# Sums of the first graph layer: GpSimd casts lanes of four bins, five bins are added as pairs, variances at the end

## The reference, cut to what matters

```python
hij = jnp.concatenate([h[src], h[dst]], axis=-1)
e = jnp.matmul(jax.nn.leaky_relu(jnp.matmul(hij, w), 0.2), a)
exp_e = jnp.exp(e)
denom = jax.ops.segment_sum(exp_e, src, num_segments=N)
out = jax.ops.segment_sum(h[src] * (exp_e / denom[src]), dst, num_segments=N)
x = _layernorm(x + out, axis=-1)
```

## Time and profile before

| | |
|---|---|
| median of 3 timed runs | 3259.38 us (3257.14 to 3259.6) |
| span of the profiled execution | 3274.5 us |
| TensorE, VectorE, ScalarE, GpSimd busy | 93%, 93%, 84%, 5% of the span |
| granted TensorE clock, mean | 0.968 |
| the stage of the change | from 1318 to 2184 us of the span |

### The profile page before, as it was taken

How to read it: one execution, slowest core, us unless ns; L and a number is a source line. 1 busy time by engine, 2 the same in 40 slices (tenths; PEclk the granted TensorE clock), 3 DMA queues, 4 the chain that set the end, 5 groups by cost and what they waited for, 6 DMA issues and landing times. The chain is left out here.

```text
span 3274.5 us, 101508 instructions
## 1 busy us (share of the span) xinstructions
PE 3060.7 (93%) x40072; PEld 2792.8 (85%) x40072; DVE 3045.9 (93%) x4921; ACT 2750.1 (84%) x6946; POOL 155.0 (5%) x249
## 2 busy tenths in 40 slices
PE   5777699999999999699999999989999999999996
PEld 4666677778777877699999999988999999999994
DVE  8999889999999997799999999989999999999997
ACT  6988888888888885799999999987888888888887
POOL 0000000000000000000000000000111111111110
PEclk9989899999999997799999999999999999999998
DMA  3000022222222222234333333334455545554541
GB/s 66 13 14 11 23 98 93 87 93 94 93 87 93 94 86 48 65 96 97 97 97 96 97 96 97 97 93 137 161 163 160 164 161 163 161 163 161 162 151 41
DMA packets 173823, 333.06 MB, mean 102 GB/s; under 512 B 54876, under 2 KB 109616, under 8 KB 173264
## 3 DMA queue, kind: packets, MB, share of 16 engines
q1 hardware_dynamic: 170996, 323.30, 32.5%
q10 hardware_dynamic: 2348, 3.20, 0.4%
HBM read 320.77 MB, written 5.66 MB: 100 GB/s over the span
## 5 line engine op out<-in xcount | busy, mean ns | idle before, releaser
L1009 PE MATMUL l_gathered<-xp,l_src_onehot 128*128 128x128 bf16 x7203 | 467.0, 221 | 11.2 <-DVE l_src_onehot L922 11.2
L1436 PE MATMUL l_gathered<-hp,l_onehot 128*128 128x128 bf16 x7203 | 458.5, 219 | 0.0
L704 PE MATMUL sc_z<-sc_onehot,pq 128*128 128x256 f32 (+1 forms) x2450 | 429.4, 298 | 23.3 <-DVE sc_leaky L617 18.3
L1009 PEld LDWEIGHTS l_gathered<-xp,l_src_onehot 128*128 128x128 bf16 x7203 | 407.9, 99 | 26.3 <-DVE l_src_onehot L922 11.7
L788 ACT ACTIVATE sc_leaky<-sc_z 128x1024 f32<-128x1024 f32 (+3 forms) x325 | 309.8, 953 | 143.3 <-PE sc_z L708 140.5
L617 DVE SCALAR_TENSOR_TENSOR sc_leaky<-sc_z,sc_leaky 128x1024 f32<-128x1024 f32 (+3 forms) x325 | 370.1, 1139 | 60.0 <-ACT sc_leaky L788 52.5
L847 DVE TENSOR_TENSOR l_lane<-iota_b,l_lane_pairs 128x896 bf16<-128x896 bf16 x686 | 421.0, 614 | 0.0
L1436 PEld LDWEIGHTS l_gathered<-hp,l_onehot 128*128 128x128 bf16 x7203 | 406.1, 98 | 0.4
L708 PE MATMUL sc_z<-sc_onehot,pq 128*128 128x256 f32 (+1 forms) x2450 | 400.9, 286 | 0.0
L1450 PE MATMUL l_acc<-e,l_lane_wide 128*128 128x132 f32 x2744 | 385.5, 283 | 0.3 <-ACT e L1514 0.3
L704 PEld LDWEIGHTS sc_z<-sc_onehot,pq 128*128 128x128 f32 x2450 | 344.6, 196 | 35.9 <-issue 34.5
(11 more groups left out here) (246 smaller groups left out, 6107.4 us busy)
## 6 DMA issues: line engine op xcount, KB each, us to landing
rows_got<-edge_rows_wide SPq DMA_DIRECT2D x338, 448.0 KB, 3.7
l_got<-edge_rows_src SPq DMA_DIRECT2D x343, 224.0 KB, 3.2
placed<-edge_rows SPq DMA_DIRECT2D x144, 512.0 KB, 3.7
out_dram<-X SPq DMA_DIRECT2D x12, 256.0 KB
S<-edge_rows_wide SPq DMA_DIRECT2D x5, 448.0 KB, 8.4
edge_rows<-e SPq DMA_DIRECT2D x98, 6.1 KB
edge_rows_wide<-e SPq DMA_DIRECT2D x98, 12.2 KB
sc_last_rows<-edge_rows SPq DMA_DIRECT2D x24, 64.0 KB, 3.5
```

Source lines behind the costliest of these rows:

```text
L704: nc.tensor.matmul(z[:, b, 0:nw, :], PQ[:, b0 + b, q, 0:C], hot[:, r % HOTS, b, 0, 0:nw, :], start=(b == u and q == 0), stop=False)
L1009: ins = nc.tensor.matmul(gps[:, t % 2, i * P:(i + 1) * P], hot[:, t % RING, i, :], parts[:, g * GX + i, q, :], start=(q == 0), stop=(q == 2))
L1436: ins = nc.tensor.matmul(gps[:, t % 2, i * P:(i + 1) * P], dst_hot[:, t % RING, i, :], hp[:, g * GX + i, q, 0:C], start=(q == 0), stop=(q ...
```

## The change

Of the 7 bins of a round, 5 instead of 4 are added as pairs of halves, and 2 instead of 3 in plain float32. VectorE still weighs 4 (`BANK`) and ScalarE 3. The lanes' cast is divided: GpSimd casts the first four bins (`WIDENED`), ScalarE the other three (`widen_late`, semaphore `late_wide`). Messages, halves and lanes get three buffers (`KEPT`), the source one-hot four. The table's split and the source one-hot go a round further ahead.

VectorE's order in an iteration is now: source one-hot of t+3, low halves of t-1, lane one-hot of t+1, weigh t, block work. TensorE gathers t+2 ahead of adding up t. ScalarE has weigh_late, widen_late, take_high.

At a block's end VectorE adds the two parts of `acc` to X by two additions in two rounds, without S and GpSimd; statistics of all blocks are kept, and after the last round seven instructions over all 49 blocks form mean and variance from them.

```diff
@@ -852,7 +852,7 @@
 def layer0_sums(nc, k, parts, xs, den, src_rows, e0, X, S, mean_var):
     NB, PER = NBK, NBK // GX
     R = NB * PER
-    RING, LOADS, SPLIT = 3, 4, 4
+    RING, LOADS, KEPT, SPLIT, BANK, WIDENED = 4, 5, 3, 5, 4, 4
     BY_SCALAR = (2, 4, 6)
     F32R = mybir.dt.float32r
     with Stage(nc) as ctx:
@@ -864,15 +864,15 @@
 
         s = {n: ctx.semaphore("l0_" + n) for n in (
             "chain", "scaled", "scaled_late", "part_high", "part_rest", "part_middle", "part_low",
-            "hot", "staged", "lane", "lane_wide", "gathered", "messages", "late_messages", "high", "low", "added", "taken", "summed", "stats")}
+            "hot", "staged", "lane", "lane_wide", "gathered", "messages", "late_messages", "high", "low", "late_wide", "added", "taken", "summed", "stats")}
         loaded = [ctx.semaphore(f"l0_loaded{h}") for h in range(LOADS)]
         rden = sb("rden", [P, k.NI])
         got = sb("got", [P, LOADS, GX * P], BF16)
         hot = sb("src_onehot", [P, RING, GX, P], BF16)
-        lane, lane_wide = sb("lane", [P, 2, GX, P], BF16), sb("lane_wide", [P, 2, GX, P], F32R)
+        lane, lane_wide = sb("lane", [P, KEPT, GX, P], BF16), sb("lane_wide", [P, KEPT, GX, P], F32R)
         lane_pairs = sb("lane_pairs", [P, 2, NB, 2], BF16)
-        msg, halves = sb("messages", [P, 2, GX, C]), sb("message_halves", [P, 2, SPLIT, 2, C], F32R)
-        stats = sb("stats", [P, 2, 6])
+        msg, halves = sb("messages", [P, KEPT, GX, C]), sb("message_halves", [P, KEPT, SPLIT, 2, C], F32R)
+        stats, apart = sb("stats", [P, NB, 6]), sb("apart", [P, NB])
         gps = ps("gathered", [P, 2, 1024])
         acc = ps("acc", [P, 2, 512])
 
@@ -925,74 +925,92 @@
                 def weigh(t):
                     n, g = divmod(t, PER)
                     dve.wait_ge(s["gathered"], t + 1)
-                    if t >= 2:
-                        dve.wait_ge(s["low"], t - 1)
-                    nc.vector.tensor_tensor(msg[:, t % 2, 0:SPLIT], gps[:, t % 2, 0:SPLIT * P].rearrange("p (i c) -> p i c", i=SPLIT),
-                                            e0[:, n, g * GX:g * GX + SPLIT].unsqueeze(2).to_broadcast([P, SPLIT, C]), ALU.mult
+                    if t >= KEPT:
+                        dve.wait_ge(s["low"], t - KEPT + 1)
+                    nc.vector.tensor_tensor(msg[:, t % KEPT, 0:BANK], gps[:, t % 2, 0:BANK * P].rearrange("p (i c) -> p i c", i=BANK),
+                                            e0[:, n, g * GX:g * GX + BANK].unsqueeze(2).to_broadcast([P, BANK, C]), ALU.mult
                                             ).then_inc(s["messages"], 1)
 
                 def take_low(t):
                     dve.wait_ge(s["high"], t + 1)
-                    nc.vector.tensor_tensor(halves[:, t % 2, :, 1, :], msg[:, t % 2, 0:SPLIT], halves[:, t % 2, :, 0, :], ALU.subtract
-                                            ).then_inc(s["low"], 1)
+                    nc.vector.tensor_tensor(halves[:, t % KEPT, :, 1, :], msg[:, t % KEPT, 0:SPLIT], halves[:, t % KEPT, :, 0, :],
+                                            ALU.subtract).then_inc(s["low"], 1)
 
                 def take(n):
                     dve.wait_ge(s["added"], (n + 1) * PER)
-                    nc.vector.tensor_reduce(S[:, n, :], acc[:, n % 2, 0:2 * C].rearrange("p (q c) -> p c q", q=2), AX.X, ALU.add
-                                            ).then_inc(s["taken"], 1)
+                    nc.vector.tensor_tensor(X[:, n, :], X[:, n, :], acc[:, n % 2, 0:C], ALU.add).then_inc(s["taken"], 1)
+
+                def take_rest(n):
+                    dve.wait_ge(s["taken"], n + 1)
+                    nc.vector.tensor_tensor(X[:, n, :], X[:, n, :], acc[:, n % 2, C:2 * C], ALU.add).then_inc(s["summed"], 1)
 
                 def measure(n):
                     dve.wait_ge(s["summed"], n + 1)
-                    nc.vector.bn_stats(stats[:, n % 2, :], X[:, n, :]).then_inc(s["stats"], 1)
-
-                def average(n):
-                    dve.wait_ge(s["stats"], n + 1)
-                    nc.vector.bn_aggr(mean_var[:, n, :], stats[:, n % 2, :])
+                    nc.vector.bn_stats(stats[:, n, :], X[:, n, :]).then_inc(s["stats"], 1)
+
+                def average():
+                    dve.wait_ge(s["stats"], NB)
+                    even, odd = stats[:, :, 0:3], stats[:, :, 3:6]
+                    ch.link(nc.vector.tensor_tensor(mean_var[:, :, 0], even[:, :, 1], odd[:, :, 1], ALU.add))
+                    ch.link(nc.vector.tensor_tensor(apart[:], even[:, :, 1], odd[:, :, 1], ALU.subtract))
+                    nc.vector.tensor_tensor(stats[:, :, 0], even[:, :, 2], odd[:, :, 2], ALU.add)
+                    ch.link(nc.vector.tensor_tensor(apart[:], apart[:], apart[:], ALU.mult))
+                    nc.vector.tensor_scalar(mean_var[:, :, 0], mean_var[:, :, 0], 0.5, None, ALU.mult)
+                    ch.link(nc.vector.scalar_tensor_tensor(out=apart[:], in0=apart[:], scalar=C / 4.0, in1=stats[:, :, 0], op0=ALU.mult,
+                                                           op1=ALU.add))
+                    nc.vector.tensor_scalar(mean_var[:, :, 1], apart[:], 1.0 / C, None, ALU.mult)
 
                 def find_lanes(t):
                     n, g = divmod(t, PER)
-                    if t >= 2:
-                        dve.wait_ge(s["lane_wide"], t - 1)
+                    if t >= KEPT:
+                        dve.wait_ge(s["lane_wide"], t - KEPT + 1)
+                        dve.wait_ge(s["late_wide"], t - KEPT + 1)
                     if g == 0:
                         dve.wait_ge(s["staged"], n + 1)
-                    compare_lanes(nc, k, lane[:, t % 2], lane_pairs[:, n % 2, g * GX:(g + 1) * GX, :]).then_inc(s["lane"], 1)
+                    compare_lanes(nc, k, lane[:, t % KEPT], lane_pairs[:, n % 2, g * GX:(g + 1) * GX, :]).then_inc(s["lane"], 1)
 
                 ch.link(nc.vector.tensor_scalar(den, den, 1.1754944e-38, None, ALU.max))
                 ch.link(nc.vector.reciprocal(rden[:], den))
                 scale(0)
                 scale(1)
                 part_rest(0)
-                for t in range(-2, R):
-                    c = t + 3
+                for t in range(-3, R + 1):
+                    c = t + 4
                     if c + 1 < PER and c + 1 not in BY_SCALAR:
                         scale(c + 1)
                     if c < PER:
                         part_rest(c)
                     if c - 1 < PER:
                         part_low(c - 1)
-                    if t + 2 < R:
-                        make(t + 2)
-                    if t >= 0:
-                        weigh(t)
+                    if t + 3 < R:
+                        make(t + 3)
+                    if t >= 1:
+                        take_low(t - 1)
                     if 0 <= t + 1 < R:
                         find_lanes(t + 1)
-                    if t >= 0:
-                        take_low(t)
+                    if 0 <= t < R:
+                        weigh(t)
                     if t >= PER and t % PER == 2:
                         take(t // PER - 1)
+                    if t >= PER and t % PER == 3:
+                        take_rest(t // PER - 1)
                     if t >= PER and t % PER == 4:
                         measure(t // PER - 1)
-                    if t >= PER and t % PER == 5:
-                        average(t // PER - 1)
                 take(NB - 1)
+                take_rest(NB - 1)
                 measure(NB - 1)
-                average(NB - 1)
+                average()
 
             @block.gpsimd
             def _(pool):
-                for n in range(NB):
-                    pool.wait_ge(s["taken"], n + 1)
-                    nc.gpsimd.tensor_tensor(X[:, n, :], X[:, n, :], S[:, n, :], ALU.add).then_inc(s["summed"], 1)
+                def widen(t):
+                    pool.wait_ge(s["lane"], t + 1)
+                    if t >= KEPT:
+                        pool.wait_ge(s["added"], t - KEPT + 1)
+                    nc.gpsimd.tensor_copy(lane_wide[:, t % KEPT, 0:WIDENED], lane[:, t % KEPT, 0:WIDENED]).then_inc(s["lane_wide"], 1)
+
+                for t in range(R):
+                    widen(t)
 
             @block.tensor
             def _(pe):
@@ -1014,22 +1032,23 @@
                     n, g = divmod(t, PER)
                     pe.wait_ge(s["late_messages"], t + 1)
                     pe.wait_ge(s["lane_wide"], t + 1)
+                    pe.wait_ge(s["late_wide"], t + 1)
                     if g == 0 and n >= 2:
-                        pe.wait_ge(s["taken"], n - 1)
+                        pe.wait_ge(s["summed"], n - 1)
                     for i in range(SPLIT, GX):
-                        nc.tensor.matmul(acc[:, n % 2, 0:C], lane_wide[:, t % 2, i, :].bitcast(F32), msg[:, t % 2, i, :],
+                        nc.tensor.matmul(acc[:, n % 2, 0:C], lane_wide[:, t % KEPT, i, :].bitcast(F32), msg[:, t % KEPT, i, :],
```

(41 more changed lines are left out.)

## The result

The changed kernel takes 3376.95 us in the median of 4 runs (3365.61 to 3387.06) against 3259.43; the ratio is 1.0361 (95% interval 1.0332 to 1.0389). It is 117.5 us slower, where 116 were forecast. The profiled executions differ by 3385.2 - 3274.5 = 110.7 us.

What follows compares the result with a forecast made beforehand. A closed VectorE-ScalarE loop was taken to bound the kernel, TensorE close behind. Over 338 steady rounds +112 us, start +3 and end +1 raise 3259.4 to 3375 us, 3.6% slower; range 3340 to 3470.

Steps and rivals of the forecast that it cites:

- The loop: Steady rounds: weighing, ScalarE's high halves, low halves, lane one-hot close in 2.753 us against 2.422, +112 us.
- The terms within: Pieces of a steady round: high halves 0.725 us on ScalarE; low halves 0.74 and lane one-hot 0.53 on VectorE.
- TensorE: Its work in a steady round falls by 0.08 to 2.31 us, leaving it idle some 0.4 us.
- Rival C: TensorE, idling, drops to half clock in a third of the rounds: 3586 us; chance 0.05.
- GpSimd's cast: Casting four lane bins hides in VectorE's 0.43 us idle gap and costs nothing if up to 0.94 us long.
- D: Length of GpSimd's lane cast of 512 elements: taken as 0.89 us, bounds 0.57 and 1.86.
- rival A: GpSimd's lane cast exceeds 0.94 us, each 0.1 us over costing 34 us: 3463 at 1.2 us; chance 0.20.
- Block work: Block-end additions and statistics on VectorE, each under 0.3 us, start in the 0.43 us gap and delay nothing.
- Start and end: First interleaved rounds and prologue +3 us (bounds -4 and +8); after the last round +1 us.
- Rival B: VectorE's low halves don't wait for ScalarE, rounds take 2.32 us: 3229 us; chance 0.07.

Runs made afterwards that it cites:

- lanes_before_low: The changed kernel with VectorE's lane one-hot of t+1 put ahead of the low halves of t-1: 3218.57 us, ratio 0.9882.
- scalar_casts_all: The changed kernel with all seven bins of lanes cast by ScalarE, none by GpSimd: 3370.95 us, ratio 1.0348.
- low_two_later: The changed kernel with VectorE taking the low halves of t-2 instead of t-1 in iteration t: 3325.50 us, ratio 1.0199.
- block_work_alone: The kernel before with only the change's block work (two additions from PSUM, statistics finished at the end): 3261.45 us, ratio 1.0008.
- low_two_later_scalar_casts: The changed kernel with low halves of t-2 in iteration t and all lanes cast by ScalarE: 3220.77 us, ratio 0.9882.

## Why the prediction was right

*The loop.* This step carried 112 of the 116 us, and it is shown: forecast 2.753 us a round, measured 2.753; forecast idle 0.43, measured 0.43; low halves 1.48 after the weighing, measured 1.48. `lanes_before_low` removes it by order alone and comes out at 2.316.

*The terms within.* High halves forecast 0.725, measured 0.725 in the mean; low halves' spacing 0.74, measured 0.74 (1905.32 to 1906.06); lane one-hot 0.53, measured 0.54.

*TensorE.* The forecast 2.31 us was right or a bit high: most of its rounds in `lanes_before_low` are 2.28 (gathers at 1900.32 and 1902.60). In after it waits 0.32 us a round by its matmuls, 0.50 by its weight loads (0.4 forecast), at a granted clock of 1.00. The wait stands ahead of the gather, whose PSUM buffer the weighing has to free: that ends at 1904.52, and the gather starts at 1904.63. Rival C didn't come.

*GpSimd's cast.* D was bounded by 0.57 and 1.86 us and taken as 0.89. It is 0.61, near the line through the two iota rows, so rival A didn't come, and there were 0.3 us to spare. Its price of nothing is shown by `scalar_casts_all`. That the two engines block each other was read from one meeting in before, with VectorE first; `low_two_later` and `lanes_before_low` show it with either engine first. The last 0.16 us of the cast lie over the first 0.16 us of the one-hot in after and cost nothing; which of the two doesn't need the shared part then is not shown.

*Block work.* Right: in the gap in after, and equal to the old in `block_work_alone`.

*Start and end.* The start was mis-sized. Counted as in the prediction, from round 4 to round 342 (1361.52 to 2291.47), the rounds take 929.95 instead of 818.58 us, 111.4 more. From the stage's first instruction on VectorE to the weighing of round 4 it is 40.7 instead of 42.0 us, so -1.3 where +3 was forecast: the prologue to the first weighing is 2.3 longer, as expected, but the four rounds after it take 22.0 instead of 25.5. From the last weighing to the next stage it is 7.3 instead of 6.0, +1.3 where +1 was forecast. Together that is 111.4. Outside the stage the two profiles differ too: the stage begins 2.5 us later, and 3.1 us are gained behind it, which the prediction didn't have. So 111.4 + 2.5 - 3.1 = 110.8, the 110.7 between the profiles to rounding. The sum of 116 was 5 us high; that the median met it to 2 us is luck.

*Rival B* was priced at 3229 us for an order in which nothing waits, and `lanes_before_low` gives 3219: it wasn't this kernel, but it was about the size of what the order hides.

What stays open is the cause of the 3.1 us behind the stage. All six kernels in which GpSimd casts lanes gain them (1085.9 to 1086.9 us from the next stage's first instruction to the end), and none of the other six does (1089.6 to 1090.8). They lie in one place, VectorE's idle time between the last instruction of the second layer and the first one behind it: 1.43 us in each of those six, 4.71 to 4.93 in the others. Before, then after:

```profile
3226.43 0.06 DVE L2323 MEMSET fin_ln_eps<- 128x1 f32 x1 [4.88 <-issue]
...
3337.18 0.06 DVE L2343 MEMSET fin_ln_eps<- 128x1 f32 x1 [1.43 <-PEq L60]
```

Why the engine gets to this instruction sooner there is not shown.

## What to carry to other kernels

When a queue is turned round so that an instruction comes "an iteration later", count the work that lies between its producer and it in the queue, not the iterations: one iteration later gained nothing here, since the producer had moved to the end of the iteration before. Behind a cast on another engine put as much independent work as the cast takes (here both one-hots, 0.81 us past the weighing's end, for 0.80 us of cast and handing over). And when a saved amount of one engine (TensorE's 0.08 us) is paid for with work on two others, ask first which of them closes the loop: the same fifth pair cost 0.24 us a round in two orders and gained 0.06 in the third.

## What the runs showed of the hardware

- VectorE and GpSimd shut each other out, and the one that starts first goes through. With GpSimd first by 0.01 to 0.02 us in `low_two_later`, VectorE's one-hot grew from 0.44 to 0.84 us; with VectorE's low halves first by 0.13 us in `lanes_before_low`, GpSimd's cast grew from 0.61 to 1.15 us, and only the first of these cost time. In three rounds of `low_two_later` the one-hot came 0.07 us before the cast: it kept its length, and the cast grew to 0.83. The low halves behind it then met the running cast and grew in their turn, from 0.81 to 1.23 us, with 1.14 instead of 0.73 to the next start; that a cast holds up low halves no row of before had shown.

```profile
1876.48 0.43 DVE L922 TENSOR_SCALAR l_src_onehot<-l_got,part 128x896 bf16<-128x896 bf16 x1
1876.84 1.23 DVE L936 TENSOR_TENSOR l_message_halves<-l_messages,l_message_halves 128x640 fp32r<-128x640 f32 x1
...
1876.55 0.83 POOL L1010 CAST l_lane_wide<-l_lane 128x512 fp32r<-128x512 bf16 x1 [2.31 <-PE l_acc L1044]
```

- Beside a weighing from PSUM neither grew (0.68 and 0.61 us in after).
- The cast of 128x512 from bfloat16 on GpSimd takes 0.61 us.
- The profile's lengths of VectorE's instructions can grow without any change of spacing. In `low_two_later_scalar_casts` the low halves read 1.22 and the lane one-hot 1.02 us, yet the next instruction starts 0.73 and 0.54 after them:

```profile
1899.18 1.22 DVE L936 TENSOR_TENSOR l_message_halves<-l_messages,l_message_halves 128x640 fp32r<-128x640 f32 x1
1899.91 1.02 DVE L847 TENSOR_TENSOR l_lane<-iota_b,l_lane_pairs 128x896 bf16<-128x896 bf16 x1
1900.45 1.09 DVE L930 TENSOR_TENSOR l_messages<-l_gathered,e 128x512 f32<-128x512 f32 x1
1901.05 0.85 DVE L922 TENSOR_SCALAR l_src_onehot<-l_got,part 128x896 bf16<-128x896 bf16 x1
1901.41 1.22 DVE L936 TENSOR_TENSOR l_message_halves<-l_messages,l_message_halves 128x640 fp32r<-128x640 f32 x1
```

  VectorE's queue never waits there, but it never waits in `lanes_before_low` either, where the same two read 0.81 and 0.60; what brings the growth is not shown. So a sum of work is to be made from starts, not from lengths.
